# Moving ScalarE's copies of a step's products between the two exponentials of the next step, in a fused attention and FP8 linear block

## What is computed

```python
x = x + attn(layernorm(x))        # 16 heads of 16 features, over 512 tokens
x = x + linear(layernorm(x))      # 256 -> 256, the input rounded to fp8 (e4m3)

qkv    = x @ qkv_w.T + qkv_b      # 256 -> 768
scores = q @ k.T * 16 ** -0.5     # per head 512 x 512
out    = softmax(scores) @ v      # per head 512 x 16, then @ proj_w.T + proj_b
```

## Time and profile before

| | |
|---|---|
| median of 3 runs | 1080.2 us (1075.93 to 1088.58) |
| profiled execution, its own time | 1080.5 us |
| its span, first to last instruction | 1078.7 us |
| TensorE matmul busy | 975.6 us, 90% |
| VectorE busy | 857.8 us, 80% |
| ScalarE busy | 707.2 us, 66% |
| GpSimd busy | 465.6 us, 43% |
| mean granted TensorE clock | 0.951 |

### The profile page before, as it was taken

The page is one execution under the profiler, slowest core; times in us unless marked ns, Lnnn a source line. Parts: engine busy times, 40 slices in busy tenths (PEclk is TensorE's granted clock), DMA queues, the critical chain, the costliest instruction groups (busy, mean ns, idle before and its releaser), DMA issues.

```text
span 1078.7 us, 16257 instructions
## 1 busy us (share of the span) xinstructions
PE 975.6 (90%) x5796; PEld 451.3 (42%) x5796; DVE 857.8 (80%) x1186; ACT 707.2 (66%) x1299; POOL 465.6 (43%) x443
## 2 busy tenths in 40 slices
PE   3487999999999999999999999999999999998894
PEld 2243334454444434444444444344444434443333
DVE  3576788888987888898988888888989888888216
ACT  3023767777685777777686777777686777766650
POOL 3121234627272463717264453727273553524242
PEclk9666999999998999999999999999999999999966
DMA  4928181745646083665638182645647181741000
GB/s 137 124 35 88 39 110 30 104 76 81 99 56 103 29 107 65 85 95 73 107 43 124 28 107 58 94 85 80 99 53 107 26 106 29 101 59 41 2 29 30
DMA packets 44288, 79.39 MB, mean 74 GB/s; under 512 B 9904, under 2 KB 13104, under 8 KB 44208
## 3 DMA queue, kind: packets, MB, share of 16 engines
q1 hardware_dynamic: 44208, 78.36, 48.5%
HBM read 18.42 MB, written 8.39 MB: 25 GB/s over the span
## 4 chain that ended last, share of the span: by engine, by line
PE 74%; ACT 14%; DVE 6%; issue 2%; DMA 2%; SPq 1%; POOL 1%; ACTq 0%; DVEq 0%; POOLq 0%
PE ps_t L455 27%; PE ps_o L487 18%; PE ps_m L369 9%; ACT pt L566 6%; PE ps_m L380 5%; PE ps_m L406 4%; PE ps_s L469 4%; ACT parts L602 4%; ACT parts L603 3%; DVE mx L684 3%; PE ps_m L437 2%; PE ps_m L353 2%; DMA ks<-parts 1%; PE ps_m L420 1%; DVE nm L700 1%
## 5 line engine op out<-in xcount | busy, mean ns | idle before, releaser
L684 DVE TENSOR_REDUCE mx<-ps_s 128x2 f32<-128x1024 f32 x512 | 616.6, 1215 | 112.4 <-PE ps_s L469 108.8
L566 ACT ACTIVATE pt<-ps_t 128x512 f32<-128x512 f32 x1024 | 558.9, 600 | 213.8 <-PE ps_t L455 205.6
L455 PE MATMUL ps_t<-qs,ks 50*128 50x512 f32 x1024 | 424.4, 474 | 44.3 <-ACT pt L566 39.1
L469 PE MATMUL ps_s<-ks,qs 48*128 48x512 f32 x1024 | 413.1, 482 | 23.6 <-DVE mx L684 12.1
L455 PEld LDWEIGHTS ps_t<-qs,ks 50*128 50x128 f32 x1024 | 168.5, 187 | 386.1 <-ACT pt L566 307.2
L487 PE MATMUL ps_o<-pt,vt 128*32 128x512 f32 x2048 | 277.7, 615 | 0.2 <-ACT pt L566 0.2
L469 PEld LDWEIGHTS ps_s<-ks,qs 48*128 48x128 f32 x1024 | 162.8, 190 | 37.6 <-DVE mx L684 19.4
L903 POOL TENSOR_TENSOR xnT_p<-xnT,xnT_p 128x512 fp32r<-128x512 f32 x30 | 38.3, 1277 | 212.7 <-ACT xnT L586 212.7
L933 POOL TENSOR_TENSOR on<-ot,rden 128x256 f32<-128x256 f32 x63 | 39.4, 626 | 174.8 <-DVE rden L743 174.8
L369 PE MATMUL ps_m<-xnT_p,wqkv_p 128*128 128x512 f32 x360 | 103.2, 423 | 1.5 <-POOL xnT_p L903 0.8
L924 POOL TENSOR_TENSOR parts<-parts 128x512 f32<-128x512 f32 x60 | 76.6, 1277 | 37.4 <-ACT parts L603 37.4
(11 more groups left out here) (94 smaller groups left out, 761.5 us busy)
## 6 DMA issues: line engine op xcount, KB each, us to landing
qs<-parts SPq DMA_DIRECT2D x192, 128.0 KB, 6.5
ks<-parts SPq DMA_DIRECT2D x192, 128.0 KB, 7.0
xin<-in_x SPq DMA_DIRECT2D x16, 512.0 KB, 4.5
xres<-in_x SPq DMA_DIRECT2D x16, 512.0 KB, 3.8
out<-h SPq DMA_DIRECT2D x15, 512.0 KB, 9.0
qs<-nmax SPq DMA_DIRECT2D x128, 8.0 KB, 4.6
pt<-in_qkv_wT SPq DMA_DIRECT2D x1, 768.0 KB, 6.6
out<-h SPq DMA_DIRECT2D x2, 256.0 KB, 2.0
```

What stands on the lines that cost most here:

```text
L455: nc.tensor.matmul(ps_t[:, g, :], ks[par][rows, slot, keys], qs[par][rows, slot, :], start=True, stop=True).then_inc(st_done, 1)
L469: done = nc.tensor.matmul(ps_s[:, s % 2, g, :], qs[par][rows, slot, queries], ks[par][rows, slot, :], start=True, stop=True)
L566: nc.scalar.activation(pt[n % 2][:, w % 2 + 2 * a, w // 2, :], ps_t[:, a, :], ACT.Exp, scale=SCALE).then_inc(exp_done, 1)
L684: dve.tensor_reduce(mx[:, t, :, s % (STEPS // 2)], ps_s[:, s % 2, :, :], AX_X, ALU.max).then_inc(max_done, 1)
```

## The change

On ScalarE, the copies that belong to step s-1 are taken in step s, behind the first exponential and ahead of the second one. The copies are the same, with the same waits, in the same order among themselves. No copy belongs to step 31, so none is left over at the end of a slot. In slots 0 and 1 there are no exponentials, and the order there is what it was. No other engine's program is touched.

```diff
--- before.py
+++ after.py
@@ -608,23 +608,27 @@
                     act.wait_ge(lin_done, 2 * b)
                 nc.scalar.copy(hqT[:].rearrange("p c n -> p (c n)"), ps_m[:].bitcast(BF16)).then_inc(hqT_ready, 1)
 
+            def copies(u, par, present, s):
+                if s == COPY_OT[1] and present(3):
+                    copy_oT(u - 3, 1)
+                if s == COPY_OT[0] and present(2):
+                    copy_oT(u - 2, 0)
+                if s in PROJECT_V and present(1):
+                    copy_v(u - 1, 1 - par, PROJECT_V.index(s))
+                if s in TRANSPOSE_X and present(0):
+                    copy_xnT(u, TRANSPOSE_X.index(s))
+                if s in PROJECT_QK and present(0):
+                    copy_qk(u, par, PROJECT_QK.index(s))
+                if s == TRANSPOSE_HQ and present(3):
+                    copy_hqT(u - 3)
+
             def slot(u, par, present):
                 for s in range(STEPS):
                     if present(2):
                         exps(u - 2, s, 0)
+                    copies(u, par, present, s - 1)
+                    if present(2):
                         exps(u - 2, s, 1)
-                    if s == COPY_OT[1] and present(3):
-                        copy_oT(u - 3, 1)
-                    if s == COPY_OT[0] and present(2):
-                        copy_oT(u - 2, 0)
-                    if s in PROJECT_V and present(1):
-                        copy_v(u - 1, 1 - par, PROJECT_V.index(s))
-                    if s in TRANSPOSE_X and present(0):
-                        copy_xnT(u, TRANSPOSE_X.index(s))
-                    if s in PROJECT_QK and present(0):
-                        copy_qk(u, par, PROJECT_QK.index(s))
-                    if s == TRANSPOSE_HQ and present(3):
-                        copy_hqT(u - 3)
 
             def finish(b):
                 copy_oT(b, 1)
```

## The result

The changed kernel took 1144.74 us (median of 4 runs, 1139.27 to 1158.24), the kernel before in the same series 1082.18 us (median of 4, 1075.93 to 1088.58). The ratio is 1.056, with a 95% interval of 1.046 to 1.067: 5.6% slower, about 61 us (63 by the medians; the ratio leaves out the execution of 1158.24 us, which is more than 1.5% above the fastest and counts as slow). The profiled execution is the fastest of the four, 1139.27 us (span 1137.5), at a mean granted clock of 0.962. The others took 1139.57, 1149.92 and 1158.24 us at 0.959, 0.948 and 0.936: the longer the time, the lower the clock. They have no profile, so where their clock fell isn't known.

The account below looks back on a forecast made before the run. TensorE's in-order work was taken as the bound (57.7 of 60 us busy per slot). Seven delays, 13.8 + 10.6 + 2.7 + 11.3 + 17.6 + 5.0 + 3.1 = 64.1 us, plus about 1, on 1080 gave 1145 us, range 1128 to 1165.

Parts of the forecast that it names:

- step 5, bank wait of the transpose of the maxima: Transpose reuses bank ps_m, waits for the later copy of V: 0.92 us in 15 slots, 13.8 us.
- steps 7 and 8, oT and V: Two copies delay the second exponential, so step 8's output projection starts later: 0.76 us in 14 slots, 10.6 us.
- steps 13 and 15, x: Step 14's second score pair 0.19 us late (2.7 us); step 16's projection waits for GpSimd, 0.81 us more (11.3 us).
- steps 17, 19, 21 and 23, Q and K: Late second exponentials hold second score pairs: 0.42 us 42 times, 17.6 us; before step 25's pair 0.36 us, 5.0 us.
- step 27, hqT: The hqT copy delays the second exponential and step 28's second score pair: 0.22 us, 3.1 us in all.
- About 1 us for the slots that are only half filled: Allowance of about 1 us added to the 64.1 us sum of the places.
- just inside: GpSimd's low part of oT would end at T+3.01, before step 8's output projection at T+3.09, and cost nothing.
- The uncertain point: Whether an exponential and a copy behind it overlap on ScalarE; without overlap 14 us more, 1159; overlap was taken.
- Faster: Rival: the first score pair's 0.19 us idle behind Q/K copies is freed, 56 places, 11 us, 1070; 3 in 100.
- Nothing: Rival: all engines but TensorE have idle time, the copies slide in it, time stays 1080; 4 in 100.
- only the bank and GpSimd waits: Rival: only step 5's bank wait and step 15's GpSimd wait are paid (13.8 + 11.3), 1105; 5 in 100.
- The rival of the clock: Rival: TensorE's pauses drop the granted clock in each of 14 slots, 67 us more, 1212; 5 in 100.

Follow-up runs that it names:

- alone (slot): Five runs, each moving one group of copies between the exponentials against the kernel before: ratios 1.012 (V), 1.011 (step 6), 1.011 (x), 1.022 (Q and K), 1.001 (oT, hqT).
- the run with Q/K alone: Only the Q and K copies (steps 16, 18, 20, 22) moved between the exponentials, against the kernel before: ratio 1.022, 23 us.
- two variants: The changed kernel with the transpose of the maxima moved to step 3 (1139.85 us), and the kernel before with only Q/K copies between the exponentials (ratio 1.022).
- one variant: Only the Q and K copies moved, behind both exponentials of the next step, against the kernel before: ratio 1.006, 7 us.

## Why the prediction was right

The time was forecast as 1145 and came as 1144.7; a number so near is luck, since single executions of the changed kernel lie up to 19 us apart. Two executions of the four had a lower clock, too, which the sum has only as a margin. What the runs show is that the steps were right, each near its own size. In us per undisturbed slot:

| place | predicted | timeline after | alone (slot) |
|---|---|---|---|
| step 5, bank wait of the transpose of the maxima | 0.92 | 0.92 | 0.88 |
| steps 7 and 8, oT and V | 0.76 | 0.80 | 0.77 |
| steps 13 and 15, x | 0.19 + 0.81 | 0.21 + 0.89 | 1.10 |
| steps 17, 19, 21 and 23, Q and K | 3 x 0.42 + 0.36 | 3 x 0.43 + 0.37 | 1.60 |
| step 27, hqT | 0.22 | 0.24 | 0.20 |
| sum | 4.52 | 4.72 | 4.55 |

The whole slot grew by 4.61; the middle column is 0.11 more, since the product behind a late start runs 0.03 to 0.05 us shorter (from the scores of step 5 to those of step 7 the slot grew by 0.87, from step 7 to step 9 by 0.77).

The two profiled executions lie 58.8 us apart and not 65. The one of before holds a slot to which the one of after has no counterpart, 4.9 us over the undisturbed ones (about 1 us of it goes with a hold-up of 2.07 us on VectorE, the rest with the clock):

```profile
323.05:388.01 64.96, 62.73 (x364) 28.62 (x362) 53.60 (x73) 44.02 (x82) 29.63 (x29) 0.92 0.50 75
```

The last stretch between two copies of hqT was 56.55 us at 0.87 before and 53.14 us at 1.00 after, 3.4 us less. Against that, the first copy of hqT came 11.9 us later (213.82 against 201.88), where two slots of 4.6 lie ahead of it. "About 1 us for the slots that are only half filled" had no row behind it; the slots say 0.95: the stretch of slot 16 went from 54.72 to 56.55 us, 1.83 more, of which 0.88 is the fifteenth bank wait, already in the sum.

The largest miss is step 15: I let the projection follow GpSimd by 0.05 us, the distance from an exponential to a matmul, and it does by 0.14. In the kernel before GpSimd ended 0.15 ahead of the projection, and I took that for slack. The row alone couldn't decide it: the second pair of step 16 started at 546.91 there, and 0.43 behind it is 547.34 too. The same error made the low part of oT "just inside" in step 8: T+3.01 and 0.14 are T+3.15, behind the 3.09 of the sum.

What I said would show in the profile did, with one size wrong: I gave the scores' waits for exponentials some 30 us more, it is 49. The list counts the whole stand of the matmul side, 0.67 us in front of a late second pair; the loss is 0.43, since the first pair now starts 0.25 us earlier (T+1.66 instead of 1.91) and makes the stand behind it that much longer. The second pair of step 16 stands as well, 0.49 us, and that costs nothing of its own, as GpSimd holds up the projection behind it.

The uncertain point that I took from the reverse order, whether an exponential and the copy behind it overlap as well, is settled by the rows: 0.49 us from start to start (555.53 to 556.02). The Trainium skill's 93 ns of overlap (ScalarE: Activation LUTs, What ACT_TABLE_LOAD costs), against 0.11 here, would have made the sum an estimated 7 us larger, counted as three handovers in each place; the rows decide for 0.11. (Step 5 has one such handover and step 27 two, so the 7 is on the high side.)

**The rivals.** "Faster" needed the second exponential over at T+2.40; it ended at T+2.77 in the prediction, and the second pair starts at T+2.83 in the trace. It named the right lever, though: the first pair's 0.19 us did go away. With the exponentials kept early and the copies of Q and K split, that lever is worth 2.3%. "Nothing" and "only the bank and GpSimd waits" are out by the run with Q/K alone, which costs 23 us without either of these waits. The rival of the clock didn't come in the changed kernel's profiled execution: 1.00 in its full slots at a TensorE share of 90%. It came in part elsewhere: as falls of 1 to 2 us in some slots of two variants, and perhaps in the two slower executions of the changed kernel (mean clock 0.948 and 0.936), for which there is no profile. The Trainium skill tells of a clock that swings when short pauses lie between groups of matmuls (TensorE: Matmul & The Clock Gate, A second HAM failure mode: psum-queue depth-cycling). The traces don't agree with it as a rule for this kernel: the changed one, which stands still the longest, has 1.00 in all twelve full slots, and the one before has 0.92 in one of them.

## What to carry to other kernels

When an engine that works in order is moved from "copy at once" to "work first, copy then", ask what it would have done in the time in which the copy ran: here it was waiting for input that didn't exist yet. One copy fitted in there almost free (the exponential behind the copy of V started at T+0.59 where T+0.53 would do), two did not (behind those of Q and K it started at T+1.26), and the move put the whole length ahead of the last exponential. Then price each place at the next instruction of the engine that sets the time (a bank, a consumer's operand, the second of two inputs), one place at a time, with the handover between just those two engines (0.05 us from ScalarE to TensorE, 0.14 from GpSimd); here such prices added up to within 0.1 us of a slot. Where there are two short copies, one in the gap and one behind the urgent work did better than both in either place.

## What was not expected of the hardware

A 128x4 instruction of VectorE took 2.31 us in place of 0.17 when it began 0.11 us after an addition of GpSimd on 128x1024, and ended with that addition to 0.02 us; half of the slots of one variant were 1.2 us longer with it, and two of the kernel before 1 us. And in slots of the same work the clock fell to its lower level around steps 25 and 26 in five of twelve, and stayed up in the others; another variant did so three times.
